# Rotary step of an attention and mixture-of-experts layer: the rotation reads q and k from the accumulator bank of their projection

## The chip, the cores and the metric

The kernel runs on one core of one Trainium2 chip. The time is device microseconds (us) of that core for one execution. A core has TensorE (PE, matrix products and transposes, which write PSUM banks of 128 partitions x 512 float32), VectorE (DVE), ScalarE (ACT), GpSimd (POOL) and SyncE (SP, which here only issues transfers). They run side by side and are ordered by semaphores alone.

## The reference, cut to what matters

```python
def attn(x, w_qkv, w_out):                       # x: 2 x 2048 x 256, 16 heads of 16
    q, k, v = split(x @ w_qkv.T)
    q, k = rope(q), rope(k)                      # x*cos + concat(-x2, x1)*sin
    a = softmax(q @ k.T / 4)
    return (a @ v) @ w_out.T

xn = layernorm(x)
s = attn(xn, w_qkv, w_out)
e = argmax(xn @ gate_w.T)                        # one of 8 experts for each token
g = silu((relu(xn @ wg[e])**2 * (xn @ wu[e])) @ wd[e])
return x + s * g
```

All of it is float32. The change lies in the line with `rope`.

## The kernel before

The 4096 tokens are 32 tiles of 128 (`NT = 32`). A **setup** makes q, k and v of all tiles. The long part behind it walks over 16 pairs of heads: scores, exponentials on ACT, maxima on DVE, weighted values. The experts are put in after the third pair. All engines' programs are written out by hand; nothing is reordered by a scheduler.

The setup has 32 slots, one for each tile t, and two more that empty the pipeline. In a slot each engine does the following, in this order:

- **PE**: `qkv(t, 0)`, the first half of the contraction of tile t (q and k into bank `2*(t % 2)`, 512 columns, L1137; v and the expert logits into the bank next to it, 264 columns, L1138); from slot 14 on a unit of early scores, `early_score(t, 0)` (two products of 512 columns, L1162, banks 6 and 7); `qkv(t, 1)`, the second half; in slots with t % 4 >= 2, up to slot 27, `turn_x` (four transposes of a coming x, L1124); `turn_q(t - 2)` (four transposes of the rotated q and k, L1149); from slot 22 on a second unit of early scores, `early_score(t, 1)`. In slot 31 a filler product (`spin(1, 0)`, L1170) precedes the latter. So slots 14 to 21 hold one unit of early scores, slots 22 to 33 two.
- **ACT**: `qkv_copy(t)`: q and k of tile t to one of four buffers `qk_s` (L564), v (L565), the logits (L566), then `qkv_out`; `xt_copy` in the slots with `turn_x` (L555); `high_part(t - 2)` (L574), which takes the transposed q and k out of bank 5; `normal`, a normalised tile of x (L540).
- **DVE**: `low_part(t - 3)` (L745), what `high_part` rounded away, then `pt_out`; `early_maximum(t, 0)`, the maximum over one unit of early scores (L752); `rotate(t - 1)` (L735), q and k times the cosines and sines, a product of 1024 columns, then `rotated`; `early_maximum(t, 1)`. In slots 0 to 7 also statistics of x.
- **POOL**: `add_turned(t)` (L987 twice) adds the two products of a rotation and gives `rope_done`, for which `turn_q` waits.

The projections have two pairs of banks: tile t takes the banks of tile t - 2, so `qkv(t, 0)` waits until these were read. The early scores have one pair of banks: each unit waits for the maximum over the unit in front of it (`e_reduced`). Every slot's `pt_out` lets SP store q and k to `parts_d`, from which the stacks `qs` and `ks` of the first heads are loaded.

Of the kernel before, what the change touches and what calls it, by code (L numbers as in the profile page):

```python
# [21 lines left out]
def layer_kernel(nc, x_in, w_in, wout_in, wg_in, wu_in, wd_in, rope_in, ident_in, rank_in, out):  # L22
# [4 lines left out]
    H, DH = 16, 16  # L27
    E, DE = 8, 64
    P = 128
    NT = B * L // P  # L30
    GT = 4
# [20 lines left out]
    QK = 2 * D  # L52
# [27 lines left out]
    with ctx:  # L80
# [3 lines left out]
        def sem(name):  # L84
            return ctx.enter_context(nc.semaphore(name))
# [31 lines left out]
        def cut(shape, dt=F32):  # L117
            n = 1
            for s in shape:
                n *= s  # L120
            words = n * (2 if dt == BF16 else 4) // 4
            flat = arena[:, at[0]:at[0] + words]
            at[0] += words
            assert at[0] <= ARENA
            if dt == BF16:
                flat = flat.bitcast(BF16)
            if len(shape) == 1:
                return flat
            names = "abcd"[:len(shape)]
            return flat.rearrange(f"p ({' '.join(names)}) -> p {' '.join(names)}", **dict(zip(names, shape)))  # L130
# [1 line left out]

        w_sb = cut([KC, QK + VG])
        xnT = [cut([KC, W]) for _ in range(2)]
        qk_s = [cut([QK]) for _ in range(GT)]
        stats = cut([NT, 6])
        tmp = cut([4, NT])
        rab = [cut([2 * QK]) for _ in range(2)]
# [61 lines left out]
        ps = ctx.enter_context(nc.psum_tensor("ps", [P, 8, 512], F32))  # L200
# [16 lines left out]
        qkv_done = sem("qkv_done")  # L217
        qkv_out = sem("qkv_out")
        rotated = sem("rotated")
# [303 lines left out]
        def _(act):  # L523
# [34 lines left out]
            def qkv_copy(t):  # L558

                o = 2 * (t % 2)  # L560
                act.wait_ge(qkv_done, t + 1)
                if t >= GT:
                    act.wait_ge(rotated, t - GT + 1)
                nc.scalar.copy(qk_s[t % GT], ps[:, o, :])  # L564
                nc.scalar.copy(v_sb[:, t:t + 1, :], ps[:, o + 1, 0:D].unsqueeze(1))  # L565
                nc.scalar.copy(logits[:, t, :], ps[:, o + 1, D:VG]).then_inc(qkv_out, 1)  # L566

# [12 lines left out]
            for t in range(NT):  # L580
                n, j = divmod(t, GT)
                qkv_copy(t)
                if j >= 2 and n + 1 < NG:
                    xt_copy(n + 1, j - 2)
                if t >= LAG:
                    high_part(t - LAG)
                if t < 2:
                    normal(GT + 2 * t)
                    normal(GT + 2 * t + 1)
                elif t + 2 * GT - 2 < NT:  # L590
                    normal(t + 2 * GT - 2)
                if t == 1:
                    root(2)
                if t == 2 * GT - 1:
                    root(3)
# [77 lines left out]
        def _(dve):  # L673
# [54 lines left out]
            def rotate(t):  # L728

                heads = QK // DH  # L730
                dve.wait_ge(qkv_out, t + 1)
                if t >= 2:
                    dve.wait_ge(rope_done, 2 * (t - 1))
                full = [P, heads, 2, DH]
                nc.vector.tensor_tensor(rab[t % 2].rearrange("p (h w d) -> p h w d", w=2, d=DH),  # L735
                                        qk_s[t % GT].rearrange("p (h o d) -> p h o d", o=1, d=DH).to_broadcast(full),
                                        turn[:, t:t + 1, :].rearrange("p o (w d) -> p o w d", w=2).to_broadcast(full),
                                        ALU.mult).then_inc(rotated, 1)

# [23 lines left out]
            for t in range(NT):  # L763
                if t > LAG:
                    low_part(t - LAG - 1)
                early_maximum(t, 0)
                if t:
                    rotate(t - 1)
                early_maximum(t, 1)
                if t == 1:  # L770
                    inverse(2)
                if t < 2 * GT:
                    statistics(XCUT[3] + 2 * t, XCUT[3] + 2 * t + 2)
                if t == 2 * GT - 1:
                    moments(3)
                    inverse(3)
                    assert count[0] == SETUP_STEPS
            for t in range(NT, NT + LAG):
                low_part(t - LAG - 1)
                early_maximum(t, 0)  # L780
                if t == NT:
                    rotate(t - 1)
                early_maximum(t, 1)
# [326 lines left out]
        def _(pe):  # L1110
# [6 lines left out]
            def turn_x(n, i):  # L1117

                pe.wait_ge(xn_ready, n + 1)
                if n or i:  # L1120
                    pe.wait_ge(xt_out, n * 2 + i)
                for j in range(2 * i, 2 * i + 2):
                    for k in range(KC):
                        last = nc.tensor.transpose(ps[:, 4, (2 * k + j % 2) * P:(2 * k + j % 2 + 1) * P],  # L1124
                                                   gate[:, n * GT + j, k * P:(k + 1) * P], ident[:])
                last.then_inc(xt_done, 1)

            def qkv(t, k):

                n, j = divmod(t, GT)  # L1130
                o = 2 * (t % 2)
                if j % 2 == 0 and k == 0:
                    pe.wait_ge(xt_out, n * 2 + 1 + j // 2)
                if t >= 2 and k == 0:
                    pe.wait_ge(qkv_out, t - 1)
                xt = xnT[n % 2][:, k, j * P:(j + 1) * P]
                nc.tensor.matmul(ps[:, o, :], xt, w_sb[:, k, 0:QK], start=(k == 0), stop=(k == KC - 1))  # L1137
                last = nc.tensor.matmul(ps[:, o + 1, 0:VG], xt, w_sb[:, k, QK:QK + VG],  # L1138
                                        start=(k == 0), stop=(k == KC - 1))
                if k == KC - 1:  # L1140
                    last.then_inc(qkv_done, 1)

            def turn_q(t):

                pe.wait_ge(rope_done, 2 * (t + 1))
                if t:
                    pe.wait_ge(pt_out, t)
                for q in range(HM):
                    last = nc.tensor.transpose(ps[:, 5, q * P:(q + 1) * P], rq[t % 2][:, q * P:(q + 1) * P], ident[:])  # L1149
                last.then_inc(pt_done, 1)  # L1150
# [16 lines left out]
            def spin(n, bank):  # L1167

                for _ in range(n):
                    nc.tensor.matmul(ps[:, bank, 0:D], ident[:], x_sb[:, 0, :], start=True, stop=True)  # L1170
# [3 lines left out]
            def early_score(slot, i):  # L1174

                units = UNITS.get(slot, ())
                if i < len(units):
                    score_early(early[0], *units[i])
                    early[0] += 1

            turn_x(0, 0)
            for t in range(NT):
                n, j = divmod(t, GT)
                qkv(t, 0)
                early_score(t, 0)
                qkv(t, 1)
                if t == 0:
                    turn_x(0, 1)
                if j >= 2 and n + 1 < NG:
                    turn_x(n + 1, j - 2)  # L1190
                if t >= LAG:
                    turn_q(t - LAG)
                if t == NT - 1:
                    pe.wait_ge(qkv_out, NT - 1)
                    spin(1, 0)
                early_score(t, 1)
            spin(SPIN, 0)
# [41 lines left out]

            pe.wait_ge(pt_out, NT)  # L1240
            pe.wait_ge(qkv_out, NT)
            pe.wait_ge(a_loaded[1], 16 * LOADS)
            pe.wait_ge(e_reduced, NU)
            for t in range(KB, AHEAD):
# [194 lines left out]
```

## Time and profile before

| | |
|---|---|
| median of 3 runs | 1527.42 us (1527.12 to 1528.42) |
| span of the profiled execution, first to last instruction | 1524.1 us; no time of it besides the span is given |
| median of the runs less that span | 3.3 us |
| PE busy | 1494.0 us (98%) |
| DVE busy | 1383.3 us (91%) |
| ACT busy | 1229.4 us (81%) |
| POOL busy | 161.7 us (11%) |
| setup, from PE's first product to its last filler behind slot 33 | 4.5 to about 150.6 us |

Busy time is the time of an engine's instructions; a PE that is busy through a stretch may still not be at its peak. An engine's idle time is put down to what released it.

### The profile page before, as it was taken

What the parts mean: (1) busy time and instruction counts of PE and PEld (TensorE: products, weight loads), DVE (VectorE), ACT (ScalarE), POOL (GpSimd) and SP (SyncE); (2) the same over time, 40 slices, a digit from 0 to 9 for tenths busy, and PEclk for the clock granted to TensorE, in tenths of its full rate; (3) what the DMA queues carried; (4) which work ended last, traced back from release to release, by engine and by line L of the source; (5) the groups of instructions that cost most, each with busy time, mean ns of one, the idle gap of its engine ahead of it and who ended that gap; (6) DMA issues with size and microseconds to landing.
All of it is one profiled execution on the core that took longest, in us unless ns stands there. A gap on an engine that the chain in (4) does not pass through costs nothing.

```text
span 1524.1 us, 35757 instructions
## 1 busy us (share of the span) xinstructions
PE 1494.0 (98%) x13325; PEld 630.1 (41%) x13325; DVE 1383.3 (91%) x1483; ACT 1229.4 (81%) x2381; POOL 161.7 (11%) x221
## 2 busy tenths in 40 slices
PE   7999999999999999999999999999999999999998
PEld 5655433333584333333333333333333333333336
DVE  6689999999747999999999999999999999999906
ACT  4553588888768888888888888888888888888891
POOL 5332423100002211000010000000000000000110
PEclk9999999999999999999999999999999999999999
DMA  5873244345253464333333342222332423333303
GB/s 189 282 198 123 62 85 86 59 74 93 61 174 80 78 130 71 47 47 47 47 47 47 47 102 44 42 42 38 46 45 41 97 37 47 47 47 47 68 13 115
DMA packets 77753, 117.72 MB, mean 77 GB/s; under 512 B 28946, under 2 KB 64146, under 8 KB 70674
## 3 DMA queue, kind: packets, MB, share of 16 engines
q1 hardware_dynamic: 71650, 103.72, 34.9%
q0 software_dynamic: 3072, 8.39, 2.2%
q10 hardware_dynamic: 2896, 3.62, 0.7%
q8 instruction: 108, 1.77, 0.6%
q14 instruction: 27, 0.22, 0.1%
HBM read 75.05 MB, written 39.71 MB: 75 GB/s over the span
## 4 chain that ended last, share of the span: by engine, by line
PE 91%; ACT 5%; issue 1%; DVE 1%; DMA 1%; SPq 0%; POOL 0%; ACTq 0%; POOLq 0%
PE ps L1221 41%; PE ps L1234 36%; ACT arena L643 3%; PE ps L1137 3%; PE ps L1396 2%; PE ps L1138 1%; PE ps L1349 1%; PE ps L1333 1%; ACT arena L608 1%; PE ps L1170 1%; PE ps L1162 1%; PE ps L1209 1%; PE ps L1149 1%; PE ps L1300 1%; PE ps L1342 0%
## 5 line engine op out<-in xcount | busy, mean ns | idle before, releaser
L643 ACT ACTIVATE arena<-ps 128x512 f32<-128x512 f32 x2048 | 1108.7, 599 | 156.7 <-PE ps L1221 76.7
L792 DVE TENSOR_REDUCE arena<-ps 128x1 f32<-128x1024 f32 x992 | 1204.6, 1220 | 23.6 <-PE ps L1209 17.6
L1221 PE MATMUL ps<-qs,ks 50*128 50x512 f32 x2048 | 734.8, 444 | 0.3 <-ACT arena L647 0.3
L1209 PE MATMUL ps<-ks,qs 48*128 48x512 f32 x1984 | 722.5, 444 | 0.0
L1234 PE MATMUL ps<-arena 128*32 128x256 f32 x8192 | 651.0, 391 | 11.8 <-ACT arena L608 7.3
L1221 PEld LDWEIGHTS ps<-qs,ks 50*128 50x128 f32 x2048 | 297.4, 185 | 415.2 <-issue 407.3
L1234 PEld LDWEIGHTS ps<-arena 128*32 128x32 f32 x8192 | 165.0, 108 | 382.5 <-issue 380.6
L1209 PEld LDWEIGHTS ps<-ks,qs 48*128 48x128 f32 x1984 | 292.3, 185 | 3.7 <-issue 2.5
L1062 POOL COPY arena<-v_sb 128x256 f32 (+1 forms) x32 | 13.2, 416 | 931.8 <-ACT arena L608 921.2
L1137 PE MATMUL ps<-arena 128*128 128x512 f32 x128 | 69.2, 623 | 0.7 <-ACT arena L555 0.7
L564 ACT COPY arena<-ps 128x512 f32<-128x512 f32 x32 | 18.7, 585 | 53.5 <-PE ps L1138 53.4
L987 POOL TENSOR_TENSOR arena<-arena 128x256 f32<-128x256 f32 x64 | 46.0, 741 | 81.5 <-DVE arena L735 81.5
L1055 POOL DMA_INDIRECT gate<-ys_d,arena x32 | 30.4, 949 | 161.8 <-DMA gate<-ys_d,arena 103.1
L752 DVE TENSOR_REDUCE arena<-ps 128x1 f32<-128x1024 f32 x32 | 39.2, 1224 | 5.3 <-PE ps L1162 4.0
L745 DVE TENSOR_TENSOR arena<-ps,arena 128x512 fp32r<-128x512 f32 x32 | 22.0, 686 | 20.3 <-ACT arena L574 20.3
L735 DVE TENSOR_TENSOR arena<-arena,turn 128x1024 f32<-128x1024 f32 x32 | 39.3, 1228 | 0.0
L1138 PE MATMUL ps<-arena 128*128 128x264 f32 x128 | 39.2, 388 | 0.0
L1043 POOL DMA_INDIRECT xs_d<-gate,arena x32 | 31.0, 968 | 69.9 <-DMA xs_d<-gate,arena 69.3
L1138 PEld LDWEIGHTS ps<-arena 128*128 128x128 f32 x128 | 24.6, 192 | 31.2 <-issue 31.2
L893 DVE TENSOR_TENSOR arena<-arena,ps 128x64 f32<-128x64 f32 x39 | 8.6, 221 | 27.9 <-ACT arena L629 27.9
L921 DVE RECIPROCAL arena<-ps 128x512 f32<-128x512 f32 x1 | 3.4, 3356 | 31.3 <-PE ps L1389 31.3
L635 ACT ACTIVATE arena<-ps 128x256 f32<-128x256 f32 x39 | 14.9, 383 | 19.0 <-PE ps L1349 19.0
(112 smaller groups left out, 569.4 us busy)
## 6 DMA issues: line engine op xcount, KB each, us to landing
qs<-parts_d SPq DMA_DIRECT2D x186, 128.0 KB, 4.5
ks<-parts_d SPq DMA_DIRECT2D x186, 128.0 KB, 5.0
parts_d<-arena SPq DMA_DIRECT2D x64, 256.0 KB, 2.6
xs_d<-arena SPq DMA_DIRECT2D x13, 384.0 KB, 3.7
arena<-xs_d SPq DMA_DIRECT2D x13, 384.0 KB, 3.8
ys_d<-arena SPq DMA_DIRECT2D x13, 384.0 KB, 2.8
onum_d<-arena SPq DMA_DIRECT2D x124, 32.0 KB
arena<-onum_d SPq DMA_DIRECT2D x3, 1024.0 KB
```

The costliest lines, as they stand in the source:

```text
L643: nc.scalar.activation(prob[kb % 2][:, c * W:(c + 1) * W], ps[:, bank, :], ACT.Exp, scale=SCALE).then_inc(exp_done[bank], 1)
L735: nc.vector.tensor_tensor(rab[t % 2].rearrange("p (h w d) -> p h w d", w=2, d=DH), qk_s[t % GT].rearrange("p (h o d) -> p h o d", o=1, d=D ...
L752: nc.vector.tensor_reduce(most[0][:, t, u:u + 1], ps[:, 6:8, :], AX.XY, ALU.max).then_inc(e_reduced, 1)
L792: nc.vector.tensor_reduce(most[head_slot][:, tile, u:u + 1], ps[:, AB + 2 * u:AB + 2 + 2 * u, :], AX.XY, ALU.max).then_inc(a_reduced[u], 1)
L987: TT(out[:, :, a, :], turned[:, :, 0, a, :], turned[:, :, 1, 1 - a, :], ALU.add).then_inc(rope_done, 1)
L1043: nc.gpsimd.indirect_dma_start(xs_d, bass.IndirectOffsetOnAxis(ap=pos[:, t:t + 1], axis=0), gate[:, t, :], None).then_inc(rows_sorted, 16)
L1137: nc.tensor.matmul(ps[:, o, :], xt, w_sb[:, k, 0:QK], start=(k == 0), stop=(k == KC - 1))
L1138: last = nc.tensor.matmul(ps[:, o + 1, 0:VG], xt, w_sb[:, k, QK:QK + VG], start=(k == 0), stop=(k == KC - 1))
L1209: ins = nc.tensor.matmul(ps[:, AB + c, :], qs[head_slot][ABASE:ABASE + KR, tile * P:(tile + 1) * P].bitcast(F32R), ks[head_slot][ABASE:ABA ...
L1221: nc.tensor.matmul(ps[:, bank, :], ks[s][at:at + KS, kb * P:(kb + 1) * P].bitcast(F32R), qs[s][at:at + KS, c * W:(c + 1) * W].bitcast(F32R ...
L1234: last = nc.tensor.matmul(ps[32 * c:32 * (c + 1), PVB, lo:hi], vst[s][:, kb, :], prob[kb % 2][:, c * W + lo:c * W + hi], start=(kb == 0 an ...
L1396: last = nc.tensor.matmul(ps[:, i % 4, t * D:(t + 1) * D], onum[:, b * KC + k, (2 * i + t) * P:(2 * i + t + 1) * P], wo_sb[:, k, :], start ...
```

## The change

The buffers `qk_s` and ACT's copy into them are gone. `rotate(t)` reads q and k of tile t from their PSUM bank, and waits for the projection (`qkv_done`) and no longer for ACT (`qkv_out`). Since the bank is now read by DVE, everything that writes it again waits for `rotated` as well: `qkv(t, 0)` waits for the rotation of tile t - 2, the filler of slot 31 for that of tile 30, and the first score after the setup for that of tile 31.

```diff
-        qk_s = [cut([QK]) for _ in range(GT)]
...
                 act.wait_ge(qkv_done, t + 1)
-                if t >= GT:
-                    act.wait_ge(rotated, t - GT + 1)
-                nc.scalar.copy(qk_s[t % GT], ps[:, o, :])
                 nc.scalar.copy(v_sb[:, t:t + 1, :], ps[:, o + 1, 0:D].unsqueeze(1))
                 nc.scalar.copy(logits[:, t, :], ps[:, o + 1, D:VG]).then_inc(qkv_out, 1)
...
             def rotate(t):
                 heads = QK // DH
-                dve.wait_ge(qkv_out, t + 1)
+                dve.wait_ge(qkv_done, t + 1)
                 if t >= 2:
                     dve.wait_ge(rope_done, 2 * (t - 1))
                 full = [P, heads, 2, DH]
                 nc.vector.tensor_tensor(rab[t % 2].rearrange("p (h w d) -> p h w d", w=2, d=DH),
-                                        qk_s[t % GT].rearrange("p (h o d) -> p h o d", o=1, d=DH).to_broadcast(full),
+                                        ps[:, 2 * (t % 2), :].rearrange("p (h o d) -> p h o d", o=1, d=DH).to_broadcast(full),
                                         turn[:, t:t + 1, :].rearrange("p o (w d) -> p o w d", w=2).to_broadcast(full),
                                         ALU.mult).then_inc(rotated, 1)
...
                 if t >= 2 and k == 0:
                     pe.wait_ge(qkv_out, t - 1)
+                    pe.wait_ge(rotated, t - 1)
...
                 if t == NT - 1:
                     pe.wait_ge(qkv_out, NT - 1)
+                    pe.wait_ge(rotated, NT - 1)
                     spin(1, 0)
...
             pe.wait_ge(pt_out, NT)
             pe.wait_ge(qkv_out, NT)
+            pe.wait_ge(rotated, NT)
```

PE's program in slot 17 before, up to the first product of slot 18 (`ps` is PSUM, `arena` holds the weights and x, `qs` and `ks` the stacks of the scores):

```order
L1137 MATMUL ps<-arena 128x512 [waits qkv_out]
L1138 MATMUL ps<-arena 128x264
L1162 MATMUL ps<-ks,qs 128x512 [waits e_reduced]
L1162 MATMUL ps<-ks,qs 128x512
L1137 MATMUL ps<-arena 128x512
L1138 MATMUL ps<-arena 128x264
L1149 MATMUL ps<-ident,arena 128x128 [waits pt_out,rope_done]
L1149 MATMUL ps<-ident,arena 128x128 x3
L1137 MATMUL ps<-arena 128x512 [waits qkv_out,xt_out]
```

The same place now:

```order
L1134 MATMUL ps<-arena 128x512 [waits rotated,qkv_out]
L1135 MATMUL ps<-arena 128x264
L1159 MATMUL ps<-ks,qs 128x512 [waits e_reduced]
L1159 MATMUL ps<-ks,qs 128x512
L1134 MATMUL ps<-arena 128x512
L1135 MATMUL ps<-arena 128x264
L1146 MATMUL ps<-ident,arena 128x128 [waits pt_out,rope_done]
L1146 MATMUL ps<-ident,arena 128x128 x3
L1134 MATMUL ps<-arena 128x512 [waits rotated,qkv_out,xt_out]
```

No product moved. The first product of a slot has one more wait, and the whole slot is queued behind it.

DVE's program before, the end of slot 16 (its rotation, of tile 15), slot 17 (the next three rows; its rotation is of tile 16) and the start of slot 18:

```order
L735 TENSOR_TENSOR arena<-arena,turn 128x1024 [waits rope_done,qkv_out]
L745 TENSOR_TENSOR arena<-ps,arena 128x4x128 [waits hi_out]
L752 TENSOR_REDUCE arena<-ps 128x1 [waits e_scored]
L735 TENSOR_TENSOR arena<-arena,turn 128x1024 [waits rope_done,qkv_out]
L745 TENSOR_TENSOR arena<-ps,arena 128x4x128 [waits hi_out]
```

And now:

```order
L731 TENSOR_TENSOR arena<-ps,turn 128x1024 [waits rope_done,qkv_done]
L741 TENSOR_TENSOR arena<-ps,arena 128x4x128 [waits hi_out]
L748 TENSOR_REDUCE arena<-ps 128x1 [waits e_scored]
L731 TENSOR_TENSOR arena<-ps,turn 128x1024 [waits rope_done,qkv_done]
L741 TENSOR_TENSOR arena<-ps,arena 128x4x128 [waits hi_out]
```

The order stayed as it was: the rotation still stands behind the maximum of its slot, and that maximum still waits for the early scores of the same slot.

## Rows read from the trace of the kernel before

**Rows 1.** The page, part 1: busy time and share of the span.
```profile
PE 1494.0 (98%) x13325; PEld 630.1 (41%) x13325; DVE 1383.3 (91%) x1483; ACT 1229.4 (81%) x2381; POOL 161.7 (11%) x221
```

**Rows 2.** PE's waits, 0 to 200 us: total us, times, longest.
```profile
PE ps L1149 <- POOL arena L987: 4.1, 1, 4.1
PE ps L1162 <- DVE arena L752: 1.3, 2, 0.7
PE ps L1149 <- DVE arena L745: 0.9, 1, 0.9
...
PE ps L1234 <- ACT arena L643: 0.3, 1, 0.3
```

**Rows 3.** Stretches of 10 us: busy time by engine, granted clock, DMA share, GB/s.
```profile
20.00:30.00 10.00, 5.91 (x24) 3.89 (x23) 7.19 (x15) 3.07 (x8) 5.28 (x6) 0.83 0.00 1
...
80.00:90.00 10.00, 10.00 (x43) 5.76 (x42) 7.22 (x9) 6.12 (x16) 4.21 (x6) 1.00 0.48 151
...
140.00:150.00 10.00, 8.58 (x40) 5.74 (x41) 8.35 (x9) 3.20 (x6) 3.51 (x6) 1.00 0.31 107
```

**Rows 4.** Groups by line and shape, 0 to 215 us: busy, mean ns, idle before.
```profile
L735 DVE TENSOR_TENSOR arena<-arena,turn 128x1024 f32<-128x1024 f32 x32 | 39.3, 1228 | 0.0
L752 DVE TENSOR_REDUCE arena<-ps 128x1 f32<-128x1024 f32 x32 | 39.2, 1224 | 5.3 <-PE ps L1162 4.0
...
L745 DVE TENSOR_TENSOR arena<-ps,arena 128x512 fp32r<-128x512 f32 x32 | 22.0, 686 | 20.3 <-ACT arena L574 20.3
...
L564 ACT COPY arena<-ps 128x512 f32<-128x512 f32 x32 | 18.7, 585 | 53.5 <-PE ps L1138 53.4
```

**Rows 5.** Timeline of PE, slot 17: start, duration, line, instructions.
```profile
75.98 1.02 PE L1137 MATMUL ps<-arena 128*128 128x512 f32 x2
...
77.38 0.50 PE L1162 MATMUL ps<-ks,qs 48*128 48x512 f32 x2
77.81 1.12 PE L1137 MATMUL ps<-arena 128*128 128x512 f32 x2
...
79.65 1.02 PE L1137 MATMUL ps<-arena 128*128 128x512 f32 x2
```

**Rows 6.** Timeline of DVE, slot 17: maximum of slot 17, rotation of tile 16.
```profile
77.92 1.23 DVE L752 TENSOR_REDUCE arena<-ps 128x1 f32<-128x1024 f32 x1
79.06 1.21 DVE L735 TENSOR_TENSOR arena<-arena,turn 128x1024 f32<-128x1024 f32 x1
```

**Rows 7.** Timeline of PE: starts of slots 15, 22, 24, 25, 31; then slot 31's filler.
```profile
68.20 1.02 PE L1137 MATMUL ps<-arena 128*128 128x512 f32 x2
...
95.21 1.02 PE L1137 MATMUL ps<-arena 128*128 128x512 f32 x2
...
104.57 1.12 PE L1137 MATMUL ps<-arena 128*128 128x512 f32 x2
...
108.88 1.13 PE L1137 MATMUL ps<-arena 128*128 128x512 f32 x2
...
135.58 1.12 PE L1137 MATMUL ps<-arena 128*128 128x512 f32 x2
...
139.36 0.60 PE L1170 MATMUL ps<-x_sb,ident 128*128 128x256 f32 x2
```

**Rows 8.** Timeline: rotation of tile 13; a maximum and the score that waited for it.
```profile
67.18 1.22 DVE L735 TENSOR_TENSOR arena<-arena,turn 128x1024 f32<-128x1024 f32 x1
...
142.79 1.23 DVE L752 TENSOR_REDUCE arena<-ps 128x1 f32<-128x1024 f32 x1 [0.53 <-PE ps L1162]
...
144.07 0.50 PE L1162 MATMUL ps<-ks,qs 48*128 48x512 f32 x2 [0.73 <-DVE arena L752]
```

**Rows 9.** Timeline: PE's slot 2, rotation of tile 0, first `turn_q`.
```profile
17.41 1.02 PE L1137 MATMUL ps<-arena 128*128 128x512 f32 x2
...
20.77 1.21 DVE L735 TENSOR_TENSOR arena<-arena,turn 128x1024 f32<-128x1024 f32 x1
...
24.71 1.11 PE L1149 MATMUL ps<-ident,arena 128*128 128x128 f32 x4 [4.09 <-POOL arena L987]
```

## The prediction

> **What bounds the kernel now.** I read the page first, then PE's waits in the setup, then the setup in stretches of 10 us, and last the timeline slot by slot. PE is busy for 98% of the span [rows 1], so what counts is whether PE gets more or less to wait for. The change touches only the 32 slots of the setup. There PE waits little: 4.1 us once for POOL, in slot 2, 0.9 us once for DVE, 1.3 us behind slot 31, and 0.3 us for ACT just behind the setup [rows 2]. From slot 3 on it is as good as full: 10.00 of 10 us at 80 to 90 us, at a granted clock of 1.00, which is the 2.4 GHz level [rows 3]. ACT is busy there for 6.12 of 10 us and DVE for 7.22. So what the change takes off ACT is taken off an engine that PE hardly waits for, and what it adds is a wait on PE, the engine that sets the end.
>
> **What goes.** The copy of q and k on ACT: 32 times 585 ns, 18.7 us in all [rows 4]. A shorter ACT chain gives `high_part`, and with it `low_part`, up to 0.5 us earlier; DVE waited 20.3 us for it [rows 4]. But PE waited for `low_part` once, 0.9 us [rows 2]: that is the most that can come back, and the copy is otherwise worth nothing, hidden behind PE's products. I count nothing for it, since the next paragraphs put DVE's rotation in that place of the wait.
>
> **What the rotation costs.** Its operand moves from SBUF to PSUM. 512 columns with a PSUM operand take 686 ns, 1024 from SBUF 1228 ns, and 1024 read from PSUM by a maximum 1224 ns [rows 4]. The difference of the first two, 542 ns, is what 512 more columns cost; added to 686 it makes 1228 ns, the same as now. Bounds: 1.21 us below (the rotation of slot 17 [rows 6]) and twice 686 = 1.37 us above. I take 1.22. The Trainium skill has it otherwise: by its page VectorE: DVE Perf Modes, in the section on the TRN2 errata, a VectorE operation has 120 fixed cycles from PSUM against 58 from SBUF, some 65 ns more at 0.96 GHz. By that page the sum below would be 13 times 0.065 = 0.8 us larger; the rows do not show such a difference.
>
> **What the new wait costs a slot.** PE may start tile t when the rotation of t - 2 is done. That rotation is DVE's work in slot t - 1, and its place there is behind the maximum over that slot's early scores, which PE makes in the middle of the same slot. So from slot 14 on the wait closes a ring: start of a slot, early scores, maximum, rotation, start of the next slot. Its length, from slot 17:
> - start to early score: 77.38 - 75.98 = 1.40 us [rows 5], and 0.10 more, since after a wait the weights are no longer loaded in front. What that costs shows in slot 17 itself: the two first parts of a product last 1.12 us where they follow a score and 1.02 us where they follow transposes [rows 5].
> - early score to maximum: 77.92 - 77.38 = 0.54 us; maximum to rotation: 79.06 - 77.92 = 1.14 us [rows 5, 6].
> - rotation: 1.22 us. From the end of a DVE instruction to PE's start: the maximum ended at 142.79 + 1.23 = 144.02 and the score began at 144.07, 0.05 us [rows 8].
>
> The sum is 1.50 + 0.54 + 1.14 + 1.22 + 0.05 = 4.45 us for each slot. Without the wait a slot takes what PE's work takes: 79.65 - 75.98 = 3.67 us in slot 17 [rows 5]. In the trace of before the rotation of tile 16 ends at 79.06 + 1.21 = 80.27, 0.6 us after slot 18 had begun [rows 5, 6]. The wait does bite, then, and since the rotation hangs on PE's own scores, PE being late moves it as well; it cannot catch up.
>
> **Sum over the slots.**
> 1. Up to slot 15. The rotation of tile 13 ended at 67.18 + 1.22 = 68.40, so slot 15 can begin at 68.45 in place of 68.20 [rows 7, 8]: 0.25. Ahead of slot 14 there is no ring, and the rotation runs early; two places are tight. In slot 2 the products that began at 17.41 must now wait for the rotation of tile 0, to 20.77 + 1.21 + 0.05 = 22.03 [rows 9]. Behind them PE waited 4.09 us for POOL, until 24.71 [rows 9]; now it does slot 2's work, 2.6 us, and one `turn_x`, 0.44 us, in that time (from slot 17: 77.81 to 79.65 holds 0.10 of weights, 1.30 of one half of the products and 0.44 of four transposes [rows 5]) and reaches the same point at about 25.2, 0.5 us late. In both cases PE has stood idle for 4 to 4.6 us, after which the clock was at its lower level for a while (mean 0.83 at 20 to 30 us [rows 3]); it starts earlier now, so the stretch at the lower level should end earlier and give some of this back. Bounds of slots 2 to 14: 0 and 1.5 us; I take 0.1, since the wait for POOL covers nearly all. Term: **0.35**.
> 2. Slots 15 to 21, seven rings: 7 x 4.45 = 31.15 us, where 95.21 - 68.20 = 27.01 were spent [rows 7]: **+4.14**.
> 3. Slots 22, 23, 26 and 27 have two units of scores and `turn_x`. PE's work there is longer than the ring (slot 24's 4.31 us, 108.88 - 104.57 [rows 7], and 0.44 for `turn_x`, 4.75), so nothing is lost but the weights of slot 22's start: **+0.10**.
> 4. Slots 24, 25, 28, 29, 30, two units and no `turn_x`: the ring of 4.45 in place of 4.31, five times 0.14: **+0.70**.
> 5. Slot 31: the filler waits for the rotation of tile 30. It began 139.36 - 135.58 = 3.78 us after the slot [rows 7] and may now after 4.45, with its weights behind: 0.67 + 0.10 = **+0.77**.
>
> Together 6.06 us. What follows is a chain through PE with waits of at most 0.3 us behind the setup [rows 2], and none of it has slack for the 6 us: the first pairs start that much later and PE stays at 98%. Queued behind the late start of a slot are `turn_x`, `turn_q` and so ACT's and DVE's work on them, SP's stores of `parts_d` and the loads of the stacks; they shift with the slots and not further.
>
> The profiled execution spans 1524.1 us; 6.1 more is 1530.2. The median of the runs is 3.3 us above that span, so 1533.5 us.
>
> **Rivals.**
> - *The banks alternate, so the reading stays hidden* (chance 0.09, no change). In the Trainium skill the page Perfetto Trace Analysis, under Optimizing Tensor Performance, has independent groups rotate through PSUM banks so that their evacuation overlaps the next group's products. Here there are two pairs of banks, and the rotation need be done only one slot later. For it: before slot 14 it is, and ACT hands `high_part` on up to 0.5 us earlier. For it to hold, the ring would have to be 4.1 us or less (0.05 of handover and 0.10 of weights gone, and 0.2 elsewhere). Then slots with `turn_x` (3.67 + 0.44 = 4.11) lose nothing, the four without it in slots 16 to 21 0.43 each, slot 31 0.3, the lead-in 0.25: 2.3 us, 1529.7. With the reading wholly hidden it is 1527.4. Against it: the rotation of tile 16 ended 0.6 us after slot 18's start.
> - *ACT's time comes through* (0.03, faster). DVE waits 20.3 us for ACT's `high_part` [rows 4]. If that wait were on the path, its 19 or so slots would give 0.27 to 0.48 us each, 5 to 9 us: about 1520. It decides only if PE waits for `low_part` in most slots; the trace has one such wait, of 0.9 us.
> - *The clock falls* (0.05, much slower). The ring leaves PE idle for 0.7 us of 4.45 in slots 16, 17, 20 and 21. If TensorE fell to the 1.2 GHz level there, the slot's 3.67 to 4.11 us of work would take up to twice as long: 7 slots at about 7.6 us are 53 us for 27, some 22 us more besides the rest, 1553. Against it: at 140 to 150 us PE was busy for 8.58 of 10 us and the clock stayed at 1.00; it fell only where PE had stood still for 4.09 us [rows 3, 9].
> - *The ring as computed* (0.83): 1533.5. Without the 0.10 us of weights in 13 rings and two starts it is 1532.0; with a rotation of 1.37 us, 13 x 0.15 = 2.0 more, 1535.5; with 1.5 us lost in the lead-in, 1.4 more, 1537. Its own range: 1531 to 1537.5.
>
> **How the numbers follow.** A difference of 0.2%, 3.05 us, is about what a measurement of this kernel can tell from none; the forecast is 6.1 us, 0.4%. The ring, and the clock, lie beyond it, with a little of the ring's case short of it: slower 0.87. No change: 0.09 of the first rival and 0.01 of the ring's low end. Faster: 0.03. The range takes the ring's bounds down to the top of the first rival: 1530.5 to 1537.5.
>
> **What would show it.** In the changed profile: no copy of 512 columns on ACT but that of `xt_copy` (L554, before L555); the rotation at 1.21 to 1.25 us; PE's waits led by its first product of a slot (L1134) waiting for the rotation (L731), over a dozen times, longest about 0.7 us but for one of over 4 us in slot 2; slot starts 4.45 us apart from slot 15 to 22; the filler of slot 31 near 145.4 us; the granted clock at 1.00 from 30 us on; and from the end of the setup on everything 6 us later, with the same durations. The prediction is wrong if slots 16 and 17 are less than 4.2 us apart, if the clock falls in the setup, or if the delay at the filler is there and gone at the end.

## The result, and the profile after

The changed kernel takes 1534.49 us (median, 1533.36 to 1535.06), the kernel before 1527.55 us on the same chip: a ratio of 1.0049, 95% interval 1.0034 to 1.0063, 6.9 us slower. The forecast was 1533.5 us.

The profiled execution of the changed kernel took 1534.10 us and spans 1532.3 us. The span of before's profile, 1524.1 us, belongs to one of its fastest executions (those timed later span 1523.9 to 1527.0 us), so the two profiles differ by 8.2 us where the medians differ by 6.9. The page of the changed kernel, part 1, the row that answers to [rows 1]:

```profile
PE 1497.5 (98%) x13325; PEld 630.8 (41%) x13325; DVE 1383.2 (90%) x1483; ACT 1218.9 (80%) x2349; POOL 160.7 (10%) x221
```

ACT has 32 instructions less and is busy for 10.5 us less. That is less than the 18.7 us that the durations of the copies add up to, because records of one engine can overlap (in e1 below a copy starts at 70.32, lasts 0.59 us, and the next instruction starts at 70.81). The groups of the page's part 5 that answer to [rows 4] (mean ns after the busy time, idle time in front, and what ended it):

```profile
L1134 PE MATMUL ps<-arena 128*128 128x512 f32 x128 | 70.0, 629 | 9.7 <-DVE arena L731 9.0
...
L748 DVE TENSOR_REDUCE arena<-ps 128x1 f32<-128x1024 f32 x32 | 39.2, 1224 | 15.2 <-PE ps L1159 14.6
...
L731 DVE TENSOR_TENSOR arena<-ps,turn 128x1024 f32<-128x1024 f32 x32 | 38.8, 1214 | 0.0
...
L741 DVE TENSOR_TENSOR arena<-ps,arena 128x512 fp32r<-128x512 f32 x32 | 22.0, 687 | 18.0 <-ACT arena L570 18.0
```

The rotation is no slower from PSUM: 1214 ns, before 1228. Both have the same median, 1215 ns; the higher mean of before comes from one rotation of 1.66 us at 48.83 us, whose cause is open. What is new stands in the first row, PE's first product of a slot waiting 9.0 us for the rotation, and in the second: DVE now waits 14.6 us for the early scores, 4.0 us before, because PE delivers them late. PE's waits from 0 to 210 us, against [rows 2]:

```profile
PE ps L1134 <- DVE arena L731: 9.0, 15, 4.5
...
PE ps L1159 <- DVE arena L748: 1.3, 2, 0.7
...
PE ps L1167 <- DVE arena L731: 0.6, 1, 0.6
PE ps L1146 <- DVE arena L741: 0.5, 1, 0.5
...
PE ps L1219 <- ACT arena L643: 0.3, 1, 0.3
```

Fifteen waits, the longest of 4.5 us in slot 2, and one of 0.6 us at the filler. The wait of 4.1 us for POOL is gone from the list; the one for `low_part` has fallen from 0.9 to 0.5 us, and that for the load of the early scores' stacks in slot 14, 0.5 us before, no longer shows. Slot 17 on PE (start, duration), up to the start of slot 18, and the same slot on DVE:

```profile
78.44 1.10 PE L1134 MATMUL ps<-arena 128*128 128x512 f32 x2 [0.61 <-DVE arena L731]
...
79.91 0.51 PE L1159 MATMUL ps<-ks,qs 48*128 48x512 f32 x2
...
82.95 1.10 PE L1134 MATMUL ps<-arena 128*128 128x512 f32 x2 [0.60 <-DVE arena L731]
```

```profile
80.45 1.22 DVE L748 TENSOR_REDUCE arena<-ps 128x1 f32<-128x1024 f32 x1 [1.27 <-PE ps L1159]
81.59 1.22 DVE L731 TENSOR_TENSOR arena<-ps,turn 128x1024 f32<-128x1024 f32 x1
```

This is the ring, to be read around: start 78.44, score 79.91, maximum 80.45, rotation 81.59 to 82.81, next start 82.95. It is 4.51 us long; [rows 5] had 3.67 for the same slot. Each engine waits for another in turn, and no engine is full. The list of waits tells less than the starts do: the slot is 0.84 us longer and PE's idle time in it is 0.6 us, since without a wait the first product starts before the record in front of it ends (in slot 17 before, the transposes run from 75.54 to 76.14 and the product starts at 75.98). The clock, in the form of [rows 3] (20 to 30 us; slots 15 to 22; slots 23 to 31):

```profile
20.00:30.00 10.00, 7.32 (x23) 4.49 (x24) 6.57 (x16) 2.22 (x6) 2.83 (x4) 0.83 0.00 1
...
68.00:106.00 38.00, 34.91 (x141) 19.44 (x140) 25.78 (x27) 15.61 (x41) 11.76 (x17) 1.00 0.62 212
106.00:147.00 41.00, 39.61 (x154) 20.89 (x153) 37.43 (x36) 12.64 (x35) 12.08 (x18) 1.00 0.56 135
```

The granted clock stays at 1.00, the 2.4 GHz level, through all of the ring. It is lower only behind the idle time of slot 2, as before (0.83 in both).

Since the first slot begins between 11.65 and 12.92 us in the profiles of this study, whatever the kernel, I count from it. The starts of slots 3, 4, 9, 15, 22 and 31 behind slot 0, from the timelines, and the start of the main part (the first score behind the setup):

| kernel | 3 | 4 | 9 | 15 | 22 | 31 | main part | median less before's |
|---|---|---|---|---|---|---|---|---|
| before | 13.96 | 18.55 | 35.75 | 56.55 | 83.56 | 123.93 | 139.00 | |
| changed | 15.50 | 18.98 | 36.46 | 57.18 | 88.80 | 130.34 | 146.22 | +6.9 |
| e1, waits alone | 15.72 | 19.21 | 37.36 | 58.46 | 90.08 | 131.61 | 147.50 | +8.6 |
| e2, copy kept | 15.57 | 19.05 | 37.24 | 58.44 | 90.05 | 131.59 | 147.48 | +9.5 |
| e3, rotation first | 15.72 | 19.20 | 36.67 | 56.95 | 83.98 | 125.42 | 141.31 | +3.3 |
| e8, values first | 14.91 | 18.39 | 35.19 | 55.64 | 83.66 | 124.37 | 140.29 | +2.4 |
| e4, changed, early start | 9.70 | 15.33 | 31.50 | 54.18 | 85.79 | 127.30 | 143.19 | +4.5 |
| e6, before, early start | 9.46 | 15.76 | 31.86 | 54.84 | 81.86 | 122.24 | 137.30 | -1.6 |
| e5, mended | 9.58 | 14.54 | 30.87 | 53.19 | 80.22 | 120.59 | 135.67 | -3.1 |

The main part's start is 7.2 us late in the changed kernel, and the median 6.9: nothing behind the setup takes any of it back. The last two columns agree to about 1 us only (e2, e3, e8). Each start is from one profile, and from it to the end the profiles take 1372.8 to 1375.5 us; two profiles of the kernel before take 1373.4 and 1374.8. So the slots are read from the traces, and differences of 1 us between medians and starts carry no meaning here. e7 and e0 were run once each and stand below.

### The profile page after: what moved, and what is told of

It reads as the page before. It is cut to its first block, busy times and chain, and to the rows that moved or that the text cites. A ratio compares the mean times of both kernels' runs of the same rounds, so it can differ in the third digit from the quotient of the medians.

```text
span 1532.3 us, 35714 instructions
## 1 busy us (share of the span) xinstructions
PE 1497.5 (98%) x13325; PEld 630.8 (41%) x13325; DVE 1383.2 (90%) x1483; ACT 1218.9 (80%) x2349; POOL 160.7 (10%) x221
## 4 chain that ended last, share of the span: by engine, by line
PE 90%; ACT 4%; DVE 3%; issue 2%; DMA 0%; ACTq 0%
PE ps L1219 41%; PE ps L1232 36%; ACT arena L639 3%; PE ps L1134 3%; PE ps L1395 1%; DVE arena L731 1%; PE ps L1348 1%; PE ps L1135 1%; PE ps L1332 1%; PE ps L1167 1%; ACT arena L604 1%; PE ps L1207 1%; PE ps L1159 1%; PE ps L1299 1%; PE ps L1110 0%
## 5 line engine op out<-in xcount | busy, mean ns | idle before, releaser
L561 ACT COPY v_sb<-ps 128x256 f32<-128x256 f32 x32 | 12.0, 374 | 75.5 <-PE ps L1135 75.5
L748 DVE TENSOR_REDUCE arena<-ps 128x1 f32<-128x1024 f32 x32 | 39.2, 1224 | 15.2 <-PE ps L1159 14.6
L731 DVE TENSOR_TENSOR arena<-ps,turn 128x1024 f32<-128x1024 f32 x32 | 38.8, 1214 | 0.0
L631 ACT ACTIVATE arena<-ps 128x256 f32<-128x256 f32 x39 | 15.0, 385 | 18.7 <-PE ps L1348 18.7
```

The lines of the kernel that those rows point to most:

```text
L748: nc.vector.tensor_reduce(most[0][:, t, u:u + 1], ps[:, 6:8, :], AX.XY, ALU.max).then_inc(e_reduced, 1)
```

## The experiments

Three theories stood against each other. **Theory 1**: the added wait closes a ring through PE's early scores and DVE's maximum and rotation. **Theory 2**: the rotation is slower, or disturbed, when it reads PSUM. **Theory 3**: ACT's shorter chain moves starts and transfers.

**e1: the waits alone.** The kernel before, with the three waits of the diff and nothing else.

```diff
+                    pe.wait_ge(rotated, t - 1)       # qkv(t, 0); the other two as in the change
```

> The kernel before with nothing but the three added waits of PE for the rotation; ACT's copy, and the rotation's reading from SBUF, stay. Theory 1 (the ring start of slot, early score, maximum, rotation, start of slot): the loss is all in these waits, +6 to +8 us over the kernel before, starts of slots 15 to 22 4.5 us apart. Theory 2 (the rotation itself is slower or disturbed when it reads PSUM): no loss here, within 1 us of the kernel before. Theory 3 (the loss comes from ACT's shortened chain, which moves transfers and starts): no loss here either.

Measured 1536.00 us against 1527.40, ratio 1.0057 (1.0043 to 1.0071): 8.6 us slower. Slots 15 to 22 start 4.51 to 4.53 us apart. Theories 2 and 3 fall as causes of the loss: it is all there with the copy in place and the rotation reading SBUF. It is even 1.3 us larger in the table than in the changed kernel: 0.9 us by slot 9 and all 1.3 by slot 15, so ahead of the ring. PE's waits of this kernel are worth a look:

```profile
PE ps L1138 <- DVE arena L735: 5.1, 2, 4.6
...
PE ps L1138 <- ACT arena L566: 4.0, 13, 0.6
```

Thirteen waits are put down to ACT's copy of the logits. They are the ring's. The timeline of PE, of DVE and of ACT around the start of slot 15:

```profile
71.33 1.10 PE L1138 MATMUL ps<-arena 128*128 128x512 f32 x2 [0.17 <-ACT arena L566]
```

```profile
69.96 1.22 DVE L735 TENSOR_TENSOR arena<-arena,turn 128x1024 f32<-128x1024 f32 x1
```

```profile
70.32 0.59 ACT L564 COPY arena<-ps 128x512 f32<-128x512 f32 x1 [1.98 <-PE ps L1139]
70.81 0.38 ACT L565 COPY v_sb<-ps 128x256 f32<-128x256 f32 x1
71.07 0.19 ACT L566 COPY arena<-ps 128x8 f32<-128x8 f32 x1
```

The rotation of tile 13 ends at 71.18, and PE starts 0.15 us behind it, just as in the changed kernel; ACT's copy (71.07 to 71.26) is of tile 14, for which slot 15 does not wait. The name in a wait is that of the event that came last before it, and here it is not the cause.

**e2: the copy kept.** The changed kernel, with an ACT copy of 512 columns in the old place.

```diff
+                nc.scalar.copy(qk_s[t % GT], w_sb[:, 0, 0:QK])
                 nc.scalar.copy(v_sb[:, t:t + 1, :], ps[:, o + 1, 0:D].unsqueeze(1))
```

> The changed kernel with a copy of 512 columns (from the weights in SBUF to unread buffers) put back in the place where ACT's copy was; the output is the same. Theory 1 and my count of nothing for the copy: within 1 us of the changed kernel, so +6.5 to +8 us over the kernel before, the ring at 4.5 us as there. Rival (the copy's removal gives something back, hidden in the sum): slower than the changed kernel by 1 to 4 us, +8 to +11 us over the kernel before. Theory 3: back to the time before, within 1 us.

Measured 1536.85 us, ratio 1.0059 (1.0045 to 1.0072). The rival's figure, then, though the interval overlaps that of the changed kernel; the trace decides: its slots are those of e1 to within 0.2 us, though its rotation reads PSUM and that of e1 reads SBUF, and it reaches the main part 1.3 us behind the changed kernel. So the removed copy is worth 1.3 us in the changed kernel, all of it ahead of slot 15 (58.44 against 57.18). (The copy put back takes 619 ns, the one removed 585; e1 has the old one and shows the same 1.3 us.) My count of nothing was wrong. The sum did not show it, because the waits ahead of slot 15 were counted too small by about as much: with the copy in place they make slot 15 1.9 us late (58.46 in e1 against 56.55), and the term for them was 0.35. Where the gain lies: with the copy kept the starts of slots 5, 9, 13 and 15 come later by 0.2, 0.4, 0.2 and 0.2 us more than in the changed kernel. Ahead of slot 14 a rotation follows `low_part`, and that follows `high_part` on ACT, so a copy of 0.6 us in front of these makes both late. Slots 5 and 13 then begin 0.15 us behind the end of the rotation that they wait for, and in the changed kernel with about 0.2 us to spare. In slot 8 it is `turn_q` that waits for `low_part`, 0.9 us against 0.5, and in slot 14 the early score for its load, 0.2 us against none.

**e3: the rotation first.** The changed kernel; in slots 14 to 21 DVE rotates before the low part and the maximum.

```diff
             for t in range(NT):
+                first = HB + 6 <= t < NT + LAG - 12
+                if first:
+                    rotate(t - 1)
                 if t > LAG:
                     low_part(t - LAG - 1)
                 early_maximum(t, 0)
-                if t:
+                if t and not first:
                     rotate(t - 1)
```

> The changed kernel with DVE's rotation as the first instruction of slots 14 to 21 in place of the third; all else and all waits stay. Theory 1: the ring is open there, slots 15 to 21 fall back to 3.67 us (4.11 with turn_x), 4.6 us of rings and 0.25 us at slot 15 come back; what is left is the slots from 22 on (1.1 us), slot 31 (0.8 us) and the lead-in (0.4 us): +2 to +2.8 us over the kernel before. Theories 2 and 3 (the reading or ACT's chain, not the place of the rotation): as the changed kernel, +6.5 to +7.5 us.

Measured 1530.67 us, ratio 1.0021 (1.0012 to 1.0030). Slots 17 and 18 on PE:

```profile
77.66 1.02 PE L1137 MATMUL ps<-arena 128*128 128x512 f32 x2
...
79.06 0.50 PE L1162 MATMUL ps<-ks,qs 48*128 48x512 f32 x2
...
81.34 1.02 PE L1137 MATMUL ps<-arena 128*128 128x512 f32 x2
```

and on DVE:

```profile
77.43 1.23 DVE L731 TENSOR_TENSOR arena<-ps,turn 128x1024 f32<-128x1024 f32 x1 [0.27 <-PE ps L1138]
78.57 0.68 DVE L741 TENSOR_TENSOR arena<-ps,arena 128x512 fp32r<-128x512 f32 x1
79.61 1.23 DVE L748 TENSOR_REDUCE arena<-ps 128x1 f32<-128x1024 f32 x1 [0.36 <-PE ps L1162]
```

Same kernel, same waits, one instruction moved: the rotation is done at 78.66 where PE needs the bank at 81.34, and the slot is back at 3.68 us. Slots 15 to 21 take 27.03 us, before 27.01, changed 31.62. From slot 22 on, where nothing was moved, the ring is still there (4.55 and 4.52 us in slots 24 and 25). Theory 1 stands; the expected +2 to +2.8 us was a little low by the median (+3.3), while the main part starts 2.3 us late.

**e8: v first.** The changed kernel; each half of a projection makes v and the logits before q and k, and only q and k wait for the rotation.

```diff
...
+                nc.tensor.matmul(ps[:, o + 1, 0:VG], xt, w_sb[:, k, QK:QK + VG], start=(k == 0), stop=(k == KC - 1))
+                if t >= 2 and k == 0:
+                    pe.wait_ge(rotated, t - 1)
+                last = nc.tensor.matmul(ps[:, o, :], xt, w_sb[:, k, 0:QK], start=(k == 0), stop=(k == KC - 1))
...
```

> The changed kernel with the two products of each half of a projection swapped: v and the logits (264 columns) first, and the wait for the rotation only in front of q and k. Theory 1: the wait comes 0.44 us of PE's work later in the slot, so the ring is 4.5 - 0.44 = 4.1 us, which is no more than the slots with turn_x take (4.11): four slots lose 0.4 us, slot 31 0.7 us, slots from 22 on and slot 15 nothing, the lead-in 0.4 us: +2.5 to +3.5 us over the kernel before. Theories 2 and 3: as the changed kernel, +6.5 to +7.5 us.

Measured 1529.78 us, ratio 1.0014 (1.0005 to 1.0023), +2.4 us, just under the range of theory 1. The slots from 24 to 30 take PE's own 4.3 and 4.7 us again, as expected; slots 15 to 23 take 37.7 us, before 36.4. The wait is the same; 0.44 us of work that needs no rotated tile now stands in front of it. The lead-in was a miss: I expected it 0.4 us behind the kernel before, and slot 15 begins 0.9 us ahead of it (55.64 against 56.55). Against the changed kernel it is 0.6 us ahead from slot 3 on, behind slot 2's wait, and 1.3 us at slot 9. So the main part starts only 1.3 us late.

**e7: the rotation first everywhere from slot 14.** The condition of e3 is `t >= HB + 6`.

> The changed kernel with the rotation first in all slots from 14 to 31, so ahead of the maximum also where a slot has two units of early scores. Theory 1 has two rings there: the bank's is open, but the scores' own ring gets the rotation and the low part between two maxima (maximum 1.14, handover and score 0.65, maximum 1.14, rotation 1.13, low part 0.6 or more: 4.7 to 4.8 us), which is more than 4.5. Slots 15 to 21 take 3.7 and 4.1 us; slots 24, 25, 28, 29, 30 take 4.7 to 4.8 us in place of 4.5. A rival that blames only the new wait of PE expects all of them at PE's own 3.7, 4.1 and 4.3 us.

One run, 1528.56 us; the main part starts 141.41 us behind slot 0, as in e3. Slots 24, 25, 28, 29 and 30 take 4.68 to 4.69 us, and PE's wait there is for the maximum. DVE's slots:

```profile
108.97 1.22 DVE L748 TENSOR_REDUCE arena<-ps 128x1 f32<-128x1024 f32 x1
110.78 1.23 DVE L748 TENSOR_REDUCE arena<-ps 128x1 f32<-128x1024 f32 x1 [0.60 <-PE ps L1162]
111.93 1.22 DVE L731 TENSOR_TENSOR arena<-ps,turn 128x1024 f32<-128x1024 f32 x1
113.06 0.68 DVE L741 TENSOR_TENSOR arena<-ps,arena 128x512 fp32r<-128x512 f32 x1
113.66 1.22 DVE L748 TENSOR_REDUCE arena<-ps 128x1 f32<-128x1024 f32 x1
```

From maximum to maximum it is 4.69 us: the bank's ring is open, and the scores' ring has become the longer one. With the rotation between the two maxima these slots took 4.51 to 4.55 us in the changed kernel, and 4.31 in the kernel before.

**e4 and e6: an early start.** What slot 2's wait is worth. DVE's first two rotations are moved ahead of the statistics of x tiles 8 to 15, and the statistics of tiles 16 to 31 start two slots later; e4 is the changed kernel with it, e6 the kernel before.

```diff
+            rotate(0)
+            rotate(1)
             dve.wait_ge(x_loaded[2], 16)
             statistics(XCUT[2], XCUT[3])
             moments(2)
...
-                if t < 2 * GT:
-                    statistics(XCUT[3] + 2 * t, XCUT[3] + 2 * t + 2)
-                if t == 2 * GT - 1:
+                if 2 <= t < 2 * GT + 2:
+                    statistics(XCUT[3] + 2 * t - 4, XCUT[3] + 2 * t - 2)
+                if t == 2 * GT + 1:
```

> The changed kernel with DVE's first two rotations moved ahead of the statistics of x tiles 8 to 15, and the statistics of tiles 16 to 31 begun two slots later. Theory 1: PE's wait of 4.5 us in slot 2 goes or shrinks to 1 or 2 us and comes partly back in slot 4, where the rotation of tile 2 now stands behind more statistics (1.5 us); the rings are untouched. 3 to 5 us below the changed kernel, +2 to +4 us over the kernel before. If slot 2's wait costs nothing because the wait for POOL takes its place, it stays at +7.

> The kernel before with the same early start (two rotations ahead of the statistics, the later statistics two slots later). The wait for POOL of 4.1 us goes and with it the stretch at the lower clock; 1 to 2 us come back as waits in slots 3 and 4: 3 to 5 us faster than the kernel before. If it is as slow as before, the start is bound by DVE's whole work and not by the place of the first rotation.

e4: 1532.19 us, ratio 1.0029 (1.0018 to 1.0041), so +4.5 us, some 2.4 us below the changed kernel and short of the expected 3 to 5. e6: 1526.12 us, ratio 0.9992 (0.9983 to 1.0001): 1.6 us faster by the medians, the interval just takes in no change, and the expected 3 to 5 us are a miss. The wait for POOL and the stretch at the lower clock are gone, as expected (the granted clock is 1.00 from 20 to 30 us, 0.83 before). The table shows where the gain went. Slot 3 begins 4.5 us early in e6, slot 4 only 2.8, slot 15 only 1.7. PE's waits of e6 name the two takers, and its ACT timeline shows the first:

```profile
PE ps L1127 <- ACT arena L555: 1.8, 1, 1.8
PE ps L1165 <- DMA ks<-parts_d: 1.6, 1, 1.6
```

```profile
25.10 0.21 ACT L534 ACTIVATE arena<-arena 128x8 f32<-128x8 f32 x1 [4.56 <-DVE arena L698]
```

ACT stands for 4.56 us, in its program of slot 1, at a square root that waits for the statistics I had moved back, and `xt_copy` is queued behind it. The second is the load of the early scores' stacks at slot 14: PE waited 0.5 us for it before, now 1.6. What is gained ahead of slot 14 runs into that load.

**e5: all mended.** The changed kernel with the early start, the rotation first in slots 14 to 21, v first, and the fillers from slot 31 on in bank 1, which needs no wait for a rotation.

```diff
                 if t == NT - 1:
                     pe.wait_ge(qkv_out, NT - 1)
-                    pe.wait_ge(rotated, NT - 1)
-                    spin(1, 0)
+                    spin(1, 1)
```

> The changed kernel with the early start, the rotation first in slots 14 to 21, v first in a projection, and the fillers from slot 31 on in bank 1, which needs no wait for the rotation. Theory 1: no ring is left and the slots take PE's own 3.7, 4.1, 4.3 and 4.7 us; what remains is the early start's gain: 3 to 5 us faster than the kernel before, as fast as that kernel with the same early start (within 1 us). If the removed copy is worth anything to a kernel without rings, it is faster than that one by up to 1.5 us.

1524.62 us, ratio 0.9983 (0.9974 to 0.9992): 3.1 us faster than the kernel before, and the fastest of the study. Every slot from 15 on takes PE's own time (3.67, 4.11, 4.31, 4.74 us), and the waits for the rotation are gone from its list:

```profile
PE ps L1165 <- DVE arena L751: 1.3, 2, 0.7
PE ps L1165 <- DMA ks<-parts_d: 1.1, 1, 1.1
PE ps L1152 <- DVE arena L744: 1.0, 2, 0.6
```

**e9: the mended kernel with the copy kept.** The edit of e2 on e5.

> The mended kernel (early start, rotation first in slots 14 to 21, v first, fillers in bank 1) with a copy of 512 columns from the weights to unread buffers put back in front of ACT's copy of v; the output is the same. If the removed copy is worth nothing once no ring is left: as the mended kernel, 2 to 4 us below the kernel before. If its worth of 1.3 us in the changed kernel (start of the main part at 146.2 against 147.5 us) does not hang on the rings: 1 to 2 us slower than the mended kernel, and as the kernel before with the early start.

1525.92 us, ratio 0.9986 (0.9977 to 0.9995), on the same chip as e5 but in another series of runs. The medians are 1.3 us apart and the intervals overlap; in the traces the main part starts 136.63 us behind slot 0, in e5 135.67. 0.5 us of that is there at slot 14 (48.37 against 47.86) and 0.5 us is a longer wait for the load. So the copy seems worth about 1 us without rings too, again ahead of slot 15; by the times alone this is not settled. Against e6 (137.30), e9 is ahead early: it begins slot 4 at 14.63 us and not 15.76. Most of this 1.1 us comes with v first, since e4, which has the reading from the bank without v first, begins slot 4 at 15.33. The other 0.4 us is what e4 gains over e6. In e6 the two moved rotations still wait for ACT's copies, and in e4 and e9 only for the projection:

```profile
17.66 1.23 DVE L731 TENSOR_TENSOR arena<-arena,turn 128x1024 f32<-128x1024 f32 x1 [0.54 <-ACT arena L566]
19.59 1.42 DVE L731 TENSOR_TENSOR arena<-arena,turn 128x1024 f32<-128x1024 f32 x1 [0.70 <-ACT arena L566]
```

These are e6's two rotations, 1.2 us of waits. That the direct reading gives the 0.4 us by ending these waits is likely and not shown by itself, since e4 also drops the copy.

**e0: the kernel before again.**

> The kernel before, unchanged, profiled once more. Shows how far two profiles of one kernel stand apart: I expect the slots 3.67, 4.11, 4.31 and 4.74 us apart as before to 0.02 us, the main part 139 to 139.5 us behind slot 0, and slot 0 itself anywhere from 11.6 to 12.9 us, since it waits for the first loads. If slot 0 begins near 12.5 us here, the changed kernel's later start was no part of the change.

1527.34 us, span 1525.6. PE's waits in slots 2 and 8, 4.1 us for POOL and 0.9 us for `low_part`, are the same to 0.1 us, and the main part starts 138.86 us behind slot 0, against 139.00 in the first profile, just short of the 139 to 139.5 expected.

Slot 0 begins at 11.98 us, between the 11.65 of the first profile and the changed kernel's 12.22. No work in front of slot 0 was changed, and e3, with the same work there, begins at 12.92: nothing ties the later start to the change.

## Why the prediction was right

The time lay 1.0 us above the forecast, inside its range, and by the mechanism forecast. Most of the sum, the rings, was right by its own working; the term up to slot 15 was near by two errors that offset each other. The terms, from the slot starts of both timelines:

| term of the sum | forecast | measured |
|---|---|---|
| 1. up to slot 15 | 0.35 | 57.18 - 56.55 = 0.63 |
| 2. seven rings, slots 15 to 21 | 4.14 | 31.62 - 27.01 = 4.61 |
| 3. slots 22, 23, 26, 27 | 0.10 | 18.90 - 18.84 = 0.06 |
| 4. slots 24, 25, 28, 29, 30 | 0.70 | 22.64 - 21.53 = 1.11 |
| 5. the filler of slot 31, and the score behind it | 0.77 | 0.73 + 0.07 = 0.80 |
| sum | 6.06 | 7.21 |

- **The ring** was found and its members were right; it was 0.06 us too short, 4.45 for 4.51. Start to score was 1.47 us (forecast 1.50), the two DVE steps as forecast (0.54, 1.14 and 1.22), the handover from DVE to PE 0.15 us and not 0.05. The 0.05 was taken from a score that waits for one semaphore; the projection waits for two, and starts 0.15 us after the rotation's end in all 15 waits and at the filler. The trace of before had the fitting row: a `turn_q` that waits for two semaphores (46.94 us) starts 0.15 us behind the `low_part` that released it. Over 12 rings that is most of what terms 2 and 4 lack: 7 times 0.06 is 0.4 and 5 times 0.07 to 0.1 is 0.4.
- **The lead-in** was given 0.1 us besides the 0.25 of slot 15's own wait, and the term of 0.35 came to 0.63. That it came so near is luck: the waits alone cost 1.9 us up to slot 15 (e1), more than the bounds of 0 and 1.5 us allowed, and the removed copy, counted at nothing, gave 1.3 us of it back. The step about slot 2 held: PE waits 4.5 us in slot 2 and none for POOL, and slot 4 begins 0.43 us late. The stretch at the lower clock came earlier, as forecast (22 to 26 us in place of 24 to 28, by stretches of 2 us). Slot 9 adds 0.3, with a wait of 0.50 us for the rotation of tile 7, which DVE does behind a chain of statistics: a place that I had not named. Slot 14 begins 0.78 us late; its wait for the load, 0.5 us before, is gone from the list and took a part back.
- **The copy counted at nothing** was wrong by 1.3 us (e2 against the changed kernel). It also passes the 0.9 us that was given as the most that can come back: only 0.4 us of it is the wait for `low_part`; most of the rest lies in waits that the change itself brought in, and at the load of slot 14.
- **The rotation from PSUM** took 1214 ns, where 1.22 us was taken. The larger fixed cost of PSUM that the Trainium skill gives (VectorE: DVE Perf Modes, section on the TRN2 errata) is not in these rows.
- **The rivals.** The overlap of the banks falls with the fifteen waits; what it lacked is shown by e3 and e8, which restore it by moving one instruction or 0.44 us of work. ACT's time did come through, but as 1.3 us and not 5 to 9. The price of the rival on the clock was added up wrongly: 7 times 7.6 us are 22 us more than the seven rings, which makes 1555.5 and not 1553; nothing hung on it. The clock stayed at 1.00 in both stretches of rings, though PE was busy only for 34.91 of 38 us in the first.
- **What lies around the span** was taken as 3.3 us; it is 1.8 (1534.10 less 1532.3). The other 1.5 us are the chance that before's profiled execution was one of the fastest. Adding the difference to the median was sound all the same.

## What to carry to other kernels

A buffer that seems a needless copy can be what cuts a ring. Before a consumer is let read a bank directly, look up where it stands in its engine's order: if work of the bank's own writer stands in front of it (here the early score and its maximum), the two engines wait for each other once every round, and the round grows to the sum of the members. The repair is then order and not speed: the reader ahead of the foreign work, or the writer's independent work ahead of the wait; and each such move has to be held against the next ring (e7).

## What the runs showed of the hardware that was not expected

- From the end of a VectorE instruction to a TensorE product that waits for it: 0.15 us where the product waits for two or more semaphores (81.59 + 1.22 = 82.81 to 82.95), 0.05 us where it waits for one (144.02 to 144.07). It goes with the number of semaphores and not with the kind of product, as far as these runs show. The product of q and k in e8's slot 2 waits for the rotation alone, its other waits standing in front of v, and starts 0.06 us behind it (22.28 to 22.34); the transposes of `turn_q`, with two waits, start 0.15 us behind `low_part` (46.79 to 46.94 before):

```profile
21.07 1.21 DVE L731 TENSOR_TENSOR arena<-ps,turn 128x1024 f32<-128x1024 f32 x1
22.34 2.07 PE L1136 MATMUL ps<-arena 128*128 128x512 f32 x2 [4.01 <-DVE arena L731]
```

```profile
46.11 0.68 DVE L745 TENSOR_TENSOR arena<-ps,arena 128x512 fp32r<-128x512 f32 x1
46.94 0.63 PE L1149 MATMUL ps<-ident,arena 128*128 128x128 f32 x4 [0.91 <-DVE arena L745]
```

- ACT's remaining instructions of the setup became shorter with the rotation on PSUM and the copy gone: the cast of `high_part` takes 590 ns (620 before), the tile of `normal` 609 ns (632 before). With the copy kept (e2) they are at 602 and 621 ns. The cause is open.
